# Selective scan: delta and the running y summed on TensorE, du replicated through DRAM, B left in PSUM

## The reference

```python
xs = stack([x0, x1, x0[..., ::-1], x1[..., ::-1]], axis=1)   # row-major, column-major, both reversed: K = 4
x_dbl = einsum('bkdl,kcd->bkcl', xs, x_proj_weight)          # -> dts (R=6), Bs (N=16), Cs (N=16)
dts = einsum('bkrl,kdr->bkdl', dts, dt_projs_weight)
A = -exp(A_logs)                                             # K x 96 x 16
delta = softplus(dts + dt_projs_bias)
def step(h, inp):                                            # over L = 4096 positions
    h = exp(d_t * A) * h + (d_t * u_t) * B_t
    y = einsum('bkdn,bkn->bkd', h, C_t)
ys = ys + Ds * xs                                            # then the four directions are added back in place
```

## Time and profile before

| | us |
|---|---|
| median of 3 runs (lowest to highest) | 6593.33 (6592.84 to 6594.92) |
| the profiled execution | 6584.0 |
| its span | 6581.8 |
| first to last scan of the selective scan | 3241.3 to 6491.2 |

### The profile page before, as it was taken

How to read it: one execution, slowest core, us unless ns; L and a number is a source line. 1 busy time by engine, 2 the same in 40 slices (tenths; PEclk the granted TensorE clock), 3 DMA queues, 4 the chain that set the end, 5 groups by cost and what they waited for, 6 DMA issues and landing times. The chain is left out here.

```text
span 6581.8 us, 69145 instructions
## 1 busy us (share of the span) xinstructions
PE 5493.3 (83%) x15890; PEld 2653.9 (40%) x15890; DVE 5359.4 (81%) x5305; ACT 2742.5 (42%) x4050; POOL 4218.5 (64%) x2650
## 2 busy tenths in 40 slices
PE   7999798976999888806788888888888888888887
PEld 2222364642666555503333333333333333333332
DVE  4768434342199999998799998999989999899997
ACT  5767434332000000002455554555545555455555
POOL 0000323223098777896788887888878888788883
PEclk9989899988999888958899998999989999899999
DMA  1000000038555666503011111111111111011111
GB/s 41 0 0 0 7 1 0 1 109 226 119 124 124 129 131 132 111 0 85 23 34 29 34 31 28 34 29 34 32 27 34 29 34 34 25 34 32 32 34 49
DMA packets 105200, 330.99 MB, mean 50 GB/s; under 512 B 19980, under 2 KB 36808, under 8 KB 91112
## 3 DMA queue, kind: packets, MB, share of 16 engines
q1 hardware_dynamic: 104936, 328.05, 20.9%
HBM read 170.81 MB, written 56.51 MB: 35 GB/s over the span
## 5 line engine op out<-in xcount | busy, mean ns | idle before, releaser
L1747 POOL TENSOR_TENSOR l_hc<-l_h,l_c_rep 128x512 f32<-128x512 f32 x1536 | 1977.7, 1301 | 292.0 <-DVE l_h L1810 265.2
L1810 DVE TENSOR_TENSOR_SCAN l_h<-l_p_da,l_h,l_bu 128x512 f32<-128x512 f32 x1344 | 1701.0, 1266 | 0.0
L1588 PE MATMUL l_p_y<-l_hc,l_y_pick 128*96 128x512 f32 x3072 | 1639.5, 616 | 17.6 <-POOL l_hc L1747 10.8
L1674 ACT ACTIVATE l_p_da<-l_p_da,l_a_neg 128x512 f32<-128x512 f32 x1536 | 1010.2, 659 | 1531.0 <-PE l_p_da L1581 1529.5
L1578 PE MATMUL l_p_du<-l_stacked,l_pick 96*128 96x512 f32 x1536 | 1200.5, 782 | 181.4 <-DVE l_bu L1800 152.9
L1146 POOL TENSOR_TENSOR l2b_prod<-l2b_v,l2b_attn 128x3136 f32<-128x3136 f32 x114 | 990.5, 8704 | 392.5 <-ACT l2b_attn L1138 369.7
L1800 DVE TENSOR_TENSOR l_bu<-l_p_du,l_b_rep 128x512 f32<-128x512 f32 x1536 | 1015.5, 661 | 18.1 <-PE l_p_da L1581 17.3
L1581 PE MATMUL l_p_da<-l_stacked,l_pick 96*128 96x512 f32 x1536 | 732.5, 477 | 253.6 <-DVE l_h L1810 247.7
L1581 PEld LDWEIGHTS l_p_da<-l_stacked,l_pick 96*128 96x128 f32 x1536 | 304.2, 198 | 930.2 <-DVE l_h L1810 841.0
L1180 DVE TENSOR_REDUCE l2b_osum<-l2b_prod 128x64 f32<-128x3136 f32 x192 | 645.9, 3414 | 2.7
L1578 PEld LDWEIGHTS l_p_du<-l_stacked,l_pick 96*128 96x128 f32 x1536 | 301.6, 196 | 737.6 <-DVE l_bu L1800 499.2
(11 more groups left out here) (241 smaller groups left out, 8380.5 us busy)
## 6 DMA issues: line engine op xcount, KB each, us to landing
l_stacked<-l_parts SPq DMA_DIRECT2D x512, 192.0 KB, 3.2
l2b_img_high<-qkv_scratch SPq DMA_DIRECT2D x192, 306.2 KB, 5.5
l2b_img_low<-qkv_scratch SPq DMA_DIRECT2D x192, 306.2 KB, 9.2
qkv_scratch<-l2a_strip SPq DMA_DIRECT2D x32, 840.0 KB, 5.1
l2b_v<-qkv_scratch SPq DMA_DIRECT2D x48, 560.0 KB, 17.0
qkv_scratch<-l2a_v_strip SPq DMA_DIRECT2D x32, 210.0 KB, 4.0
x_front<-x SPq DMA_DIRECT2D x4, 1536.0 KB, 18.6
x_scratch<-x_front SPq DMA_DIRECT2D x4, 1536.0 KB, 14.6
```

The costliest lines, as they stand in the source:

```text
L1588: pe.matmul(p_y[par][:], y_pick[:, g, :], hc[:, g % HCS, :], start=(g == 0), stop=(g == G - 1)).then_inc(s_ymm, 1)
L1674: act.activation(p_da[g % DAS][:], p_da[g % DAS][:], ACT.Exp, scale=a_neg[:, k * G + g:k * G + g + 1]).then_inc(s_da, 1)
L1747: pool.tensor_tensor(hc[:, g % HCS, :], h[:, g, :], c_rep[:, par, :], ALU.mult).then_inc(s_hc, 1)
L1810: dve.tensor_tensor_scan(h[:, g, way], p_da[g % DAS][:, way], bu[:, g % DAS, way], state, ALU.mult, ALU.add).then_inc(s_h, 1)
```

## The change

Delta: ACT's |x|, relu, exp, 1+e, (1+e)-1 and log stay. POOL makes only the rest of e (`rest`). PE then sums relu(x), the rest and the log in PSUM by three products with an identity (`delta_sum`), and ACT copies the sum out twice, as `dd` and as the high part. Only delta goes through high and low parts, `restack` (four DMAs of 96 KB) and the replication on PE. du = dd times x is stored to a DRAM scratch (192 KB), and SP reads it back twelve times a step with a source that names each row 16 times, 256 KB a group, into a ring of 8 buffers. B stays in PSUM (`p_b`, 2 buffers, in the place of `p_du`), and DVE multiplies `du_rep` by it. Groups are taken in the order `GRP` (0, 4, 8, 1, 5, 9, ...), so that three in a row go to three different 32-row strips of `p_y`: three products with a 32-column matrix (`y_triple`). The running y is one more product (`y_whole`: the diagonal Ds matrix times x for k = 0, identity times `y_sum` else), and ACT writes `p_y` out (`take_y`), in direction 3 straight into X. `delta` and `add_y` leave DVE. ACT turns x in eight pieces during direction 0. Steps run across images, with no image start or end. A new `clear_semaphores` block on POOL stands ahead of the attention's last part.

```diff
-    HCS = 6
+    HCS = 8
+    BUS = 3
+    RING = 8
+    GRP = [(i % YT) * YJ + i // YT for i in range(G)]   # YT = 3, YJ = TRIPLES = 4
+        y_pick = sb("l3_y_pick", [128, YJ, YT * DL + DL])
+        p_b = [ps(f"l3_p_b{i}", [128, N]) for i in range(2)]
 SP:
+            def store_du(m, par):
+                sp_.wait_ge(s_du, m + 1 + DU0)
+                sp_.wait_ge(s_bu, G * (m - 1) + BU0)
+                sp_.dma_start(du_d[par], du[:]).then_inc(s_dus, 16)
+            def replicate_du(n, par, i):
+                if i == 0:
+                    sp_.wait_ge(s_dus, 16 * (n + 1) + DUS0)
+                sp_.wait_ge(s_bu, G * n + (i + 1 - RING) + BU0)
+                src = du_d[par, GRP[i] * DL:(GRP[i] + 1) * DL]
+                src = bass.AP(src.tensor, src.offset, [[0, S], [N, DL], [1, N]])
+                sp_.dma_start(du_rep[:, ring_at(par, i)], src).then_inc(s_dur[ring_at(par, i)], 16)
+            def step(n, par, more):
+                for i in range(RING, G):
+                    replicate_du(n, par, i)
+                    if more and i == RING:
+                        store_du(n + 1, 1 - par)
+                    if more and i == RING + 1:
+                        sp_.wait_ge(s_rep, G * n)
+                        restack(n + 1, 1 - par)
+                if more:
+                    for i in range(RING):
+                        replicate_du(n + 1, 1 - par, i)
 PE:
+            def delta_sum(m, copied):
+                pe.wait_ge(s_ccp, copied + CCP0)
+                pe.wait_ge(s_relu, m + 1)
+                pe.matmul(p_bc[0:C, :], ident[:], relu_x[:], start=True, stop=False)
+                pe.wait_ge(s_rest, m + 1)
+                pe.matmul(p_bc[0:C, :], ident_r[:], rest_e[:], start=False, stop=False)
+                pe.wait_ge(s_log, m + 1)
+                pe.matmul(p_bc[0:C, :], ident[:], log_e[:], start=False, stop=True).then_inc(s_d, 1)
+            def y_triple(n, t, par):
+                pe.wait_ge(s_hc, G * n + YT * t + YT + HC0)
+                for q in range(YT):
+                    mm = pe.matmul(p_y[par][q * 32:(q + 1) * 32, :], y_pick[:, t, :],
+                                   hc[:, (G * par + YT * t + q) % HCS, :], start=(t == 0), stop=False)
+                mm.then_inc(s_ymm, 1)
             def step(b, n, k, c, par, n1, n2, before):
+                for i in range(G):
+                    replicate(n, i, par)          # delta only; waits for scan i - 3
+                    if before and i == 0:  y_triple(n - 1, 2, 1 - par)
+                    if n2 and i == 1:      dt_mm(n + 2, *n2, n + 1)
+                    if n1 and i == 2:      b_mm(n + 1, 1 - par, *n1)
+                    if before and i == 3:  y_triple(n - 1, 3, 1 - par)
+                    if before and i == 4:  y_whole(n - 1, *before, 1 - par)
+                    if n1 and i == 5:      c_mm(n + 1, *n1, n2)
+                    if i == 6:             y_triple(n, 0, par)
+                    if n2 and i == 8:      delta_sum(n + 2, n + 2)
+                    if i == 9:             y_triple(n, 1, par)
 ACT:
+            def delta_and_high(m, par):
+                act.wait_ge(s_d, m + 1)
+                act.wait_ge(s_du, m + DU0)
+                act.wait_ge(s_lo, m + LO0)
+                act.activation(dd[:], p_bc[0:C, :], ACT.Identity, bias=ln_one[:])
+                restacked(m - 1, 1 - par)
+                act.activation(parts[:, 0, :], p_bc[0:C, :], ACT.Identity, bias=ln_one[:]).then_inc(s_hi, 1)
             # step, behind decay(n, k, i): 2 abs_relu(n+2), 3 exp, 4 one_plus and kept, 5 log_1e,
             # 6 c_copy(n+1), 7 take_y(n-1), 8 (k = 0) turn_x, 10 delta_and_high(n+2)
 POOL:
             def step(b, n, k, c, par, n1, n2, before):
+                for i in range(G):
+                    if n1 and i == 0:  low(n + 1, 1 - par)
+                    if n1 and i == 2:  delta_u(n + 1, *n1)
+                    times_c(n, i, par)
+                    if n2 and i == 6:  rest(n + 2)
 DVE:
+                dve.tensor_tensor(bu[:, i % BUS, :], du_rep[:, ring_at(par, i)], p_b[par][:], ALU.mult).then_inc(s_bu, 1)
                 for i in range(G):
                     times_b(b, n, i + 1, par)     # or the next step's group 0
                     scan(n, k, c, i, par)
-                    if g == 7: add_y(n - 1, *ahead(k, c, -1), 1 - par)
-                    if n2 and g == 9: delta(n + 2)
```

More of the change, by code:

```diff
@@ L1509, in all_steps, with at, image @@
[L1509 to L1517, removed]
+            if 0 <= at < STEPS:
+                return b, at // CHUNKS, at % CHUNKS
+            return None if at >= STEPS and last else (b + at // STEPS, at % STEPS // CHUNKS, at % CHUNKS)
+        def all_steps(step):
+            def at(b, k, c, par, last, eng=None):
+                first = isinstance(b, int) and b == 0 and k == 0 and isinstance(c, int) and c == 0
+                step(b, b * STEPS + (k * CHUNKS) + c, k, c, par, ahead(b, k, c, 1, last), ahead(b, k, c, 2, last),
+                     None if first else ahead(b, k, c, -1, last))
+            def image(eng, b, last):
@@ L1533, in restack @@
             def restack(m, par):
[L1535 to L1540, removed]
+                sp_.wait_ge(s_lo, m + 1 + LO0)
+                sp_.nop(nofuse=True)
+                for part in range(2):
                     for q in range(PARTS):
@@ L1714, in _ @@
+                    if k == 0 and isinstance(c, int) and c < 2 and i == 9:
+                        turn_x(b, 2 * c + 1)
+            for m in range(2):
+                abs_relu(m, 0)
+                exp_x(m)
+                one_plus(m)
+                kept(m)
+                log_1e(m)
+                delta_and_high(m, m)
+                if m == 0:
+                    c_copy(0, 0)
+            all_steps(step)(act)
+            take_y(B * STEPS - 1, B - 1, K - 1, CHUNKS - 1, 1)
         @block.gpsimd
@@ new lines, in times_c, with step @@
+            def times_c(n, i, par):
+                if i == 0:
+                    pool.wait_ge(s_ccp, n + 1 + CCP0)
+                pool.wait_ge(s_h, G * n + i + 1 + H0)
+                pool.wait_ge(s_ymm, TRIPLES * n + (i - HCS) // YT + 1 + YMM0)
+                pool.tensor_tensor(hc[:, (G * par + i) % HCS, :], h[:, i, :], c_rep[:, par, :], ALU.mult).then_inc(s_hc, 1)
+            def step(b, n, k, c, par, n1, n2, before):
+                if k == 0 and isinstance(c, int) and c == CHUNKS - 1:
+                    pool.wait_ge(s_xt, CHUNKS * b + CHUNKS)
+                    pool.nop(nofuse=True)
+                for i in range(G):
+                    if n1 and i == 0:
+                        low(n + 1, 1 - par)
+                    if n1 and i == 2:
+                        delta_u(n + 1, *n1)
+                    times_c(n, i, par)
+                    if n2 and i == 6:
+                        rest(n + 2)
@@ L1776, in _ @@
+            rest(0)
+            low(0, 0)
+            delta_u(0, 0, 0, 0)
+            rest(1)
+            all_steps(step)(pool)
         @block.vector
@@ new lines, in scan, with step @@
+                dve.wait_ge(s_bu, G * n + i + 1 + BU0)
+                state = 0.0 if isinstance(c, int) and c == 0 else h[:, i, first:first + 1]
+                dve.tensor_tensor_scan(h[:, i, way], p_da[i % DAS][:, way], bu[:, i % BUS, way],
+                                       state, ALU.mult, ALU.add).then_inc(s_h, 1)
+            def step(b, n, k, c, par, n1, n2, before):
+                for i in range(G):
+                    if i < G - 1:
+                        times_b(b, n, i + 1, par)
+                    elif n1:
+                        times_b(b, n + 1, 0, 1 - par)
+                    scan(n, k, c, i, par)
@@ L1854, in channel_norm_out @@
+            times_b(0, 0, 0, 0)
+            all_steps(step)(dve)
+            dve.wait_ge(s_y, B * STEPS + Y0)
 def channel_norm_out(nc, w, X, out):
```

473 lines of the change are left out of this document (238 added, 235 removed).

## The result

The changed kernel takes 6394.26 us (median of 4 runs, 6389.84 to 6410.51) against 6594.12 (4 runs, 6592.84 to 6600.80): a ratio of 0.9699, 95% interval 0.9686 to 0.9712. The forecast was 6365, its range 6180 to 6600.

The account below looks back on a forecast made before the run. DVE, never resting, was taken as the bound. Scan stage 3250 falls to 2708 plus 307 of stalls, 3015, 235 less; 5 for the ends leaves 230; 6584.0 becomes 6354, plus 9 for the median 6363, rounded 6365; range 6180 to 6600.

Parts of the forecast that it names:

- What leaves DVE: Delta, `add_y`, the image end and their waits leave DVE's scan stage: 542 us at most.
- the floor: DVE's scan and `times_b` pairs, 1.77 us apart, sum to 2708 us over the scan stage, 21.24 a step.
- The new wait: PE's `delta_sum` waits for POOL's `rest`, so DVE stalls before scan 9: 1.5 us a step at full clock, 2.4 in all.
- The clock term: PE at 1.2 GHz once a step after the wait for `rest`: 0.9 us taken, between nothing and 3.0.
- The triple: Three y products on PE between replications: 1.72 us taken, bounds 0.86 and 2.58; 1.08 by the Trainium skill.
- The drain: Switching tiling mode drains TensorE: estimated 0.16 a switch, 8 switches a step, 1.3 us of PE, about 40 us in all.
- scan 10 is 0.2 late again: DVE's scan 10 waits 0.2 us because the triple between replications 9 and 10 takes 1.72.
- Rival 1: The wait for `rest` costs nothing; DVE at 21.24 to 21.7 us a step, 6060 to 6120 us. Chance 0.12.
- Rival 2: PE becomes the bound: triples in a row, pause, 1.2 GHz; 24.5 to 25.4 us a step, 6500 to 6600. Chance 0.17.
- Rival 3: Replicas arrive late by DMA, slower than before from 147 GB/s down; 7030 us at 130 GB/s. Chance 0.12.
- Rival 4: Waits on ring, `p_b` and sum take on DVE what delta and `add_y` took: 6560 to 6620 us. Chance 0.05.
- Ends: Outside the stalls: start +6 us, semaphore-clearing block +3, last chunk about 4 sooner; 5 us in all.

Follow-up runs that it names:

- Experiment 9: The changed kernel with `delta_sum` behind replication 10 and y products one behind the other, without column groups: 6070.88 us; 6061.61 in a second run.
- experiment 3: The changed kernel with the relu product of `delta_sum`, ahead of the wait for `rest`, run four times instead of once: 6308.74 us.
- experiment 2: The changed kernel with `delta_sum` moved behind replication 10 on PE and ACT's copies one group later: 6120.42 us; 6130.36 in a second run.
- experiments 9 and 10: The second of these: the changed kernel with `delta_sum` behind replication 10, column groups kept, each triple of y products run three times: 6071.75 us.
- experiment 4: The changed kernel without column groups, each y product 96 rows wide and one behind the other, wait kept: 6622.55 us.

## Why the prediction was right, and where it was off

**What leaves DVE, and the floor.** Right in kind: only `times_b` and the scan are left, no gap between images. The floor of 2708 us was taken from pairs 1.77 apart; the stage without its 321.3 us of stalls (324.8 less the 3.5 ahead of its first scan) is 2738.3, 30 us more. The scan took 1280 ns on average where the profile of before has 1266, 19 us in 1344 scans:

```profile
L1810 DVE TENSOR_TENSOR_SCAN l_h<-l_p_da,l_h,l_bu 128x512 f32<-128x512 f32 x1344 | 1701.0, 1266 | 0.0
```

Experiment 9 comes within 14 us of the floor: 3262.0 to 5984.3 is 2722 us.

**The new wait.** This was the heart of the prediction and held: place (scan 9), releaser (ACT's decay, behind PE, behind POOL's `rest`), the 3.1 us in which PE waits, once in each step. The stall was put at 2.4 us a step and is 321.3 / 128 = 2.51. In the step shown, counted from the end of scan 6 at 3998.45 (scan 8 starts at 4000.72, two pairs of 1.77 after scan 6), `rest` ends at 2.58 (forecast 2.6), PE takes it at 2.73 (2.85), and scan 9 starts at 6.48. The forecast of 5.25 at full clock plus 0.9 is 6.15.

**The clock term.** Taken at 0.9, and too small. In this step the replication leaves PE at 5.57 instead of 4.47, 1.1 for the clock, and the steps of experiment 3 in which PE is not late put it at 1.3 for scan 9. Those steps also confirm the sum at full clock: scan 9 at 5.16, forecast 5.25. The mechanism holds. The reason for the choice, that the low stretch begins in the pause, is in the windows (0.50 already between 3998.00 and 4001.10), but the stretch lasts to about 4004.8: it covers the whole pause and then all of rest, log and replication 9, and spares only part of the triple.

**The triple.** Mis-sized: 1.72 was taken, 1.06 is what three take at full clock, nearly as little as one product alone (1.02). They run beside each other. The Trainium skill (TensorE: Matmul & The Clock Gate, row and column tiling) gives a speedup of 2.38, from which 1.08 was worked out; the same three in a row last 2.74 in experiment 9, a speedup of 2.6. The drain that the Trainium skill describes (TensorEngine Tiling (Array Packing), Key Properties) was estimated at 0.16 a switch. By the modelled starts it is smaller, but not nothing. The triple at 4006.69 begins 0.06 before the modelled end of the replication ahead of it (4006.26 + 0.49), and a product without column groups begins 0.16 before:

```profile
3996.74 0.50 PE L1644 MATMUL l_p_da<-l_stacked,l_pick 96*128 96x512 f32 x1 [1.28 <-DVE l_h L1917]
3997.08 1.02 PE L1634 MATMUL l_p_bc<-l_relu_x,l_ident 96*96 96x512 f32 x2
```

That is 0.1 a switch; no run isolates it. The term "scan 10 is 0.2 late again" came out in size (23.6 / 128 = 0.18) and not by its reason: at full clock a triple of 1.06 leaves no such wait (none ahead of scan 10 in experiment 3), and it is the low clock that brings it: in the steps in which scan 10 is late the triple behind the wait takes 1.73 (median), by chance what was taken for it at full clock.

**Rival 1** fell: the wait cost 274 us (experiment 2). Its price of 6060 to 6120 is about the time of the kernels without the wait (6120 and 6130 with column groups, 6062 to 6072 in experiments 9 and 10). **Rival 2** is refuted for the change. Its parts, triples in a row behind the pause and at a low clock, come together in experiment 4: 6622.55, where 6500 to 6600 was forecast. But PE is not the bound even there, since experiment 9 has the same products and no wait and takes 6070.88. **Rival 3** is refuted: 0.61 of the DMA engines were busy, less than the 0.7 to 0.85 forecast. 3.74 MB in a step of 23.9 us is 156 GB/s, the number of the window, and where the engines are full they move 244 to 246 GB/s in this stage, more than the 212 of the earlier trace rows that the forecast went by. The margin of 2 us for the tightest replica was not needed, DVE waits for `du_rep` only at the start (21.1 us in two waits). **Rival 4**, as told, did not come.

**Ends.** Start +6 and semaphores +3 were forecast, +3.5 is measured for both; the end gave 2.0 where 4 was forecast. Together 1.5 more instead of 5.

**How much of the near hit is luck.** The profiled execution was forecast at 6354 and took 6394.9, 41 more: 30 from the floor, 14 from the stall, 3.5 less from the ends. The median was forecast 9 above that execution, rounded up by 2, and lies 0.6 below it. These 11 us, which nothing in the kernel stands for, bring the miss from 41 down to 29. Within the stall the clock term was too small, and the 0.1 for ACT's two copies is nearly missing (0.8 us ahead of scan 11 in the whole stage). The upper bound of the stall, 3.9, is not what its terms give: 1.5 and 3.0 are 4.5, by which the prediction's own range would end at 6634 instead of 6555. The result lies inside by either.

What the prediction did not contain is that the clock is not only a price of the wait. It costs DVE another 60 us of idle time after the wait is gone, in a kernel whose PE has slack, and the column groups, which make PE faster, are what brings it about. Nor does it take a long pause: in experiment 2 PE's pauses are 1.28 us at most but for two, and about a third of the stage is at 1.2 GHz. Why the low stretch falls on the critical chain in some steps and not in others stays open.

## What to carry to other kernels

When work moves to another engine, follow what its first instruction waits for through the queues of both engines: here one wait, set two groups too early, ate 274 of 542 us, and moving the consumer behind it gave them back, while issuing the producer one group earlier gave 166. When the engine that bounds is fed by TensorE, compare granted clocks before saving TensorE time: a form that is 2.6 times faster was worth 228 us beside a wait and cost 60 without it. A test of a resource (a smaller ring) has to be read in its trace and not by its time alone, since here it measured the order of a queue.

## What the runs showed of the hardware that was not expected

- Three float32 products on 32-column groups, 128x512 each, take 1.06 us at full clock, one takes 1.02, three in a row 2.74. Going from a product without groups to one with groups costs about 0.1.
- In the step shown, TensorE's granted clock is 0.50 from about 3998.0, when the last product ahead of a pause is just ending, through the pause (3998.1 to 4001.2) and 3.6 us of work behind it, to about 4004.8. It is also at 0.50 where there is no long pause: busy for 3.00 of 3.00 us in experiment 2, behind pauses of at most 1.28.
- Work on TensorE that is of no use made a kernel some 55 us faster.
- DVE's `scalar_tensor_tensor` of 96x512 takes 1.65 us beside a running product of POOL and 0.72 when it starts first, POOL's then taking 1.72 instead of 1.27.
- Loads that read one DRAM row sixteen times reached 216 GB/s over 2000 us, and up to 246 in windows of 1 us inside the changed kernel's wait.
